# Sorting products and skip connection of a graph network: scaling, attention vectors and bias on other engines

## What is computed

```python
def _L0_gnn_ref(x, edge_index, W_gat, att_src, att_dst, gat_bias, bn_gamma, bn_beta, W_skip, b_skip):
    identity = x @ W_skip + b_skip
    h = (x @ W_gat).reshape(N, H, C)              # N 1250, H 8, C 64
    a_src = jnp.einsum('nhc,hc->nh', h, att_src)
    a_dst = jnp.einsum('nhc,hc->nh', h, att_dst)
    ...                                            # softmax over edges, sum, batch norm, gelu
    return out + identity
x = _layernorm(x + _L0_gnn_ref(x, edge_index, ...), axis=-1)
```

## Time and profile before

| | us |
|---|---|
| median of 3 runs (lowest, highest) | 2041.71 (2039.19, 2046.14) |
| the profiled execution, device time | 2038.94 |
| its span, first to last instruction | 2036.9 |

### The profile page before, as it was taken

The page is one execution under the profiler, slowest core; times in us unless marked ns, Lnnn a source line. Parts: engine busy times, 40 slices in busy tenths (PEclk is TensorE's granted clock), DMA queues, the critical chain, the costliest instruction groups (busy, mean ns, idle before and its releaser), DMA issues.

```text
span 2036.9 us, 21846 instructions
## 1 busy us (share of the span) xinstructions
PE 1693.8 (83%) x5296; PEld 870.4 (43%) x5296; DVE 1607.7 (79%) x3252; ACT 895.4 (44%) x1833; POOL 527.2 (26%) x597
## 2 busy tenths in 40 slices
PE   2668888788387777479999999999598998999997
PEld 1445545533133333444444444457353443444443
DVE  9997899889899999789999999987665754762222
ACT  0112555666355454457777777763204423441100
POOL 4777870044000000045455555520000000002000
PEclk9788999988698899789999999998799999999999
DMA  5101000123210010154545454530010111111000
GB/s 166 10 6 8 6 5 1 36 101 110 103 39 35 32 42 0 56 150 140 151 135 155 133 154 136 153 74 1 25 42 21 62 62 62 58 56 52 0 25 25
DMA packets 66428, 133.78 MB, mean 66 GB/s; under 512 B 19156, under 2 KB 22752, under 8 KB 66385
## 3 DMA queue, kind: packets, MB, share of 16 engines
q1 hardware_dynamic: 40561, 70.33, 11.1%
q0 software_dynamic: 22080, 56.10, 10.3%
q10 hardware_dynamic: 3744, 6.82, 0.9%
HBM read 117.78 MB, written 15.24 MB: 65 GB/s over the span
## 4 chain that ended last, share of the span: by engine, by line
DVE 39%; PE 38%; issue 15%; DMA 4%; DVEq 3%; ACT 2%; SPq 0%; POOL 0%; ACTq 0%; POOLq 0%
PE PS L954 15%; DVE arena L1492 5%; PE PS L922 4%; PE PS L1002 4%; DVE arena L1608 4%; PE PS L738 3%; DVE arena L1488 3%; DVE arena L1353 3%; DVE arena L1604 3%; DVE arena L1611 2%; DVE arena L1614 2%; DVE arena L1352 2%; DVE arena L1383 2%; PE PS L998 2%; PE PS L990 2%
## 5 line engine op out<-in xcount | busy, mean ns | idle before, releaser
L852 PE MATMUL PS<-arena 128*125 128x512 f32 x832 | 397.1, 600 | 20.4 <-ACT arena L1196 20.3
L954 PE MATMUL PS<-arena 128*125 128x512 f32 x720 | 314.5, 600 | 12.2 <-ACT arena L1262 6.6
L1195 ACT ACTIVATE arena<-arena,gslot 128x128 f32<-128x128 f32 x624 | 204.4, 390 | 136.6 <-DVE arena L1608 129.0
L800 PE MATMUL PS<-arena 125*128 125x512 f32 (+1 forms) x480 | 196.3, 552 | 79.0 <-DVE arena L1492 78.9
L597 POOL DMA_INDIRECT arena<-xup,gidx x208 | 218.1, 1048 | 88.4 <-issue 50.0
L561 POOL DMA_INDIRECT recs<-arena x170 | 211.1, 1242 | 62.1 <-issue 47.7
L852 PEld LDWEIGHTS PS<-arena 128*125 128x125 f32 x832 | 152.2, 188 | 157.5 <-issue 101.3
L954 PEld LDWEIGHTS PS<-arena 128*125 128x125 f32 x720 | 136.8, 190 | 189.3 <-issue 189.3
L847 PE MATMUL PS<-w4r,h3r 128*128 128x512 f32 x211 | 168.2, 797 | 10.3 <-DVE h3r L1627 10.3
L800 PEld LDWEIGHTS PS<-arena 125*128 125x128 f32 x480 | 90.3, 199 | 185.1 <-DVE arena L1492 102.4
L1148 ACT ACTIVATE arena<-arena,c 125x1250 f32<-125x1250 f32 x80 | 107.0, 1337 | 137.6 <-DVE arena L1488 137.4
(11 more groups left out here) (235 smaller groups left out, 2905.9 us busy)
## 6 DMA issues: line engine op xcount, KB each, us to landing
arena<-in_spline_wT SPq DMA_DIRECT2D x16, 1024.0 KB, 5.3
arena<-h_rows SPq DMA_DIRECT2D x104, 128.0 KB, 3.4
arena<-uv_rows SPq DMA_DIRECT2D x18, 610.4 KB
h_rows<-arena ACTq DMA_DIRECT2D x26, 256.0 KB, 2.1
arena<-as_rows SPq DMA_DIRECT2D x8, 610.4 KB
arena<-xup,gidx POOLq DMA_INDIRECT x208, 4.2
recs<-arena POOLq DMA_INDIRECT x170, 2.6
x_sb<-in_x SPq DMA_DIRECT2D x1, 2500.0 KB
```

Source lines behind the costliest of these rows:

```text
L800: ins = t.matmul(PS[:, 3 * par + q, 0:n1 - n0], hs[:, sblk, par * C:par * C + 2 * C], wt[:, sblk % WR, n0:n1], start=(sblk == 0), stop=(sb ...
L852: ins = t.matmul(PS[:NP, 2 + 2 * par + q, :], w[:, k, :], prod[:, k, q * 512:(q + 1) * 512], start=(k == 0), stop=(k == GT - 1))
L954: ins = t.matmul(PS[:NP, b, :], basis[:, slot, (k * HB + b) * NP:(k * HB + b + 1) * NP], w_sp[:, slot, k * D:(k + 1) * D], start=(first an ...
L1195: A(pr[:, 4 + m, :], pr[:, 8, :], ACT.Copy, scale=y[:, 1 + m:2 + m])
```

## The change

Five things are changed.

1. Sort rounds: VectorE writes one plain one-hot of the lane per column (`lane_oh`, a new tile), the tile one-hot, and then 6 of the 10 `lane_src` tiles as one-hot times source. ScalarE writes all 10 `lane_dl` tiles and the other 4 `lane_src` tiles (`ACT_SRC = 4`) as a copy with a per-partition scale (`scale_lanes`). `sort_batch` waits for both engines.
2. wa: TensorE transposes W_gat in rounds 4 and 5, ScalarE copies it to `wgT`, and 16 products with 16 columns in round 6 give wa. The attention vectors are loaded into a zeroed block layout `att_d` by 16 DMAs of 64 four-byte pieces.
3. The first layer's blocks run one round later (b = j - 5), and one row part moves behind the rounds.
4. Skip: VectorE adds the identity to W_skip once, in round 10; the bias is a row in a zeroed tile, added by a fifth product with ones; ScalarE copies the sum from PSUM over `x_sb`. Both additions of VectorE go.
5. `cnt_d` is cleared by GpSimd at the start; some semaphores of the loads are joined.

```diff
@@ sync
-            sp.dma_start(att_b[:, 0, :], bass_row(a["L0_gnn_att_src"].rearrange("h c -> (h c)"), 128)).then_inc(s_wg_in, 16)
-            sp.dma_start(att_b[:, 1, :], bass_row(a["L0_gnn_att_dst"].rearrange("h c -> (h c)"), 128)).then_inc(s_wg_in, 16)
+            for q, name in enumerate(("L0_gnn_att_src", "L0_gnn_att_dst")):
+                for h in range(H):
+                    p0 = (h % 2) * C
+                    sp.dma_start(att_d[p0:p0 + C, h // 2, q * H + h:q * H + h + 1], a[name][h:h + 1, :].rearrange("h c -> c h"))\
+                      .then_inc(s_w0_in, 16)
+            sp.dma_start(b_rows[0:1, :], a["L0_gnn_b_skip"].rearrange("(a n) -> a n", a=1)).then_inc(s_w0_in, 16)
@@ gpsimd
+            pool.memset(att_d, 0.0)
+            pool.memset(b_rows, 0.0)
+            pool.memset(cnt_d[:], 0).then_inc(s_const0, 1)
@@ tensor
             def sort_batch(j):
                 pe.wait_ge(s_sort_ok, j + 1)
+                pe.wait_ge(s_lane_cp, j + 1)
+            def w_transposed(c):
+                if c >= 2:
+                    pe.wait_ge(s_wa_cp, c - 1)
+                for k in range(KT):
+                    ins = t.transpose(PS[:, 2 + c % 2, k * 128:(k + 1) * 128], w_gat[:, k, c * 128:(c + 1) * 128], ident[:])
+                ins.then_inc(s_wt_ps, 1)
             for j in range(ROUNDS):
                 sort_batch(j)
-                b = j - 4
+                b = j - 5
+                if j == 4:
+                    pe.wait_ge(s_w0_in, 16 * (3 + 2 * H))
+                    w_transposed(0)
+                    w_transposed(1)
+                if j == 5:
+                    w_transposed(2)
+                    w_transposed(3)
+                if j == 6:
+                    pe.wait_ge(s_wa_cp, KT)
+                    for m in range(KT):
+                        for c in range(KT):
+                            ins = t.matmul(PS[:, 2, m * 2 * H:(m + 1) * 2 * H], wgT[:, c, m * 128:(m + 1) * 128], att_d[:, c, :],
+                                           start=(c == 0), stop=(c == KT - 1))
+                    ins.then_inc(s_wt_ps, 1)
...
-                if j >= ROUNDS - 2:
-                    row_part(j - (ROUNDS - 2))
+                if j == ROUNDS - 1:
+                    row_part(0)
+            row_part(1)
             row_part(2)
+            def skip_block(b):
+                if b >= 2:
+                    pe.wait_ge(s_skip_cp, b - 1)
+                t.matmul(PS[:NP, 6 + b % 2, :], ones[:, 0:NP], b_rows, start=True, stop=False)
+                for k in range(KT):
+                    ins = t.matmul(PS[:NP, 6 + b % 2, :], xT[:, k, b * NP:(b + 1) * NP], w_skip[:, k, :], start=False, stop=(k == KT - 1))
+                ins.then_inc(s_skip_ps, 1)
@@ scalar
+            def scale_lanes(j):
+                act.wait_ge(s_lane_ok, j + 1)
+                if j >= 2:
+                    act.wait_ge(s_order_ps, j)
+                for n in range(SB):
+                    r, c = (j % 2) * SB + n, j * SB + n
+                    ins = A(lane_dl[:, r, :], lane_oh[:, r, :], ACT.Copy, scale=dl1[:, c:c + 1])
+                    if n >= SB - ACT_SRC:
+                        ins = A(lane_src[:, r, :], lane_oh[:, r, :], ACT.Copy, scale=rec[:, c, R_SRCF:R_SRCF + 1])
+                ins.then_inc(s_lane_cp, 1)
-            for b in range(NB + 1):
+            for j in range(ROUNDS):
+                scale_lanes(j)
+                b = j - 5
+                if j in (4, 5):
+                    w_transposed(2 * (j - 4))
+                    w_transposed(2 * (j - 4) + 1)
+                if j == 6:
+                    act.wait_ge(s_wt_ps, KT + 1)
+                    A(wa[:].rearrange("p k n -> p (k n)"), PS[:, 2, 0:KT * 2 * H], ACT.Copy).then_inc(s_wa_cp, 1)
+                if b < 0 or b > NB:
+                    continue
                 if b < NB:
                     act.wait_ge(s_xt_ps, b + 1)
                     A(xT[:, :, b * NP:(b + 1) * NP],
...
+            for b in range(NB):
+                count_groups(4 * b, 2)
+                act.wait_ge(s_skip_ps, b + 1)
+                A(x_sb[:, b, :], PS[:NP, 6 + b % 2, :], ACT.Copy).then_inc(s_skip_cp, 1)
@@ vector
                 for n in range(SB):
-                    v.tensor_scalar(lane_src[:, r, :], iota_src[:NP, 0:128], lane, rec[:, c, R_SRCF:R_SRCF + 1], ALU.is_equal, ALU.mult)
-                    v.tensor_scalar(lane_dl[:, r, :], iota_src[:NP, 0:128], lane, dl1[:, c:c + 1], ALU.is_equal, ALU.mult)
-                    ins = v.tensor_scalar(tile_oh[:, r, :], iota_src[:NP, 0:NT], tile_f[:, c:c + 1], None, ALU.is_equal)
+                    ins = v.tensor_scalar(lane_oh[:, r0 + n, :], iota_src[:NP, 0:128], lane_f[:, c0 + n:c0 + n + 1], None, ALU.is_equal)
+                ins.then_inc(s_lane_ok, 1)
+                for n in range(SB):
+                    v.tensor_scalar(tile_oh[:, r0 + n, :], iota_src[:NP, 0:NT], tile_f[:, c0 + n:c0 + n + 1], None, ALU.is_equal)
+                dve.wait_ge(s_lane_ok, j + 1)
+                for n in range(SB - ACT_SRC):
+                    ins = v.tensor_scalar(lane_src[:, r0 + n, :], lane_oh[:, r0 + n, :], rec[:, c0 + n, R_SRCF:R_SRCF + 1], None, ALU.mult)
                 ins.then_inc(s_sort_ok, 1)
-                if j == 8:
-                    gat_vectors()
+                if j == 10:
+                    dve.wait_ge(s_w0_in, 16 * (3 + 2 * H))
+                    for k in range(KT):
+                        d = w_skip[:, k, k * 128:(k + 1) * 128]
+                        v.tensor_tensor(d, d, ident[:], ALU.add)
-            link(v.memset(cnt_d[:], 0))
-                v.tensor_tensor(x_sb[:, b, :], x_sb[:, b, :], PS[:NP, 6 + b % 2, :], ALU.add).then_inc(s_skip_cp, 1)
-                v.tensor_tensor(x_sb[:, b, :], x_sb[:, b, :], b_skip_b, ALU.add)
```

More of the change, by code:

```diff
@@ L29 @@
 WR = 5
+ACT_SRC = 4
 LEAD = 2
@@ L149, in build @@
         assert o[0] <= 12000
-        b_skip_b = at(12000, [NP, D])
+        b_rows = at(12000, [128, D])
         xT = at(13000, [128, KT, N])
         w_gat, w_skip = at(18000, [128, KT, D]), at(20048, [128, KT, D])
-        att_b = at(22096, [128, 2, D])
+        att_d = at(22096, [128, KT, 2 * H])
+        wgT = at(26000, [128, KT, D])
         h_sb = at(23120, [NP, NB, D])
@@ L172, in build @@
         dl1 = at(5800, [NP, EC])
+        lane_oh = at(10620, [NP, 2 * SB, 128], f16)
         lane_src = at(1020, [NP, 2 * SB, 128], f16)
@@ L256, in build @@
         s_basis_ok = sem("s_basis_ok")
-        s_bn_in = sem("s_bn_in")
         s_bn_ok = sem("s_bn_ok")
@@ L342, in build @@
         s_sort_ok = sem("s_sort_ok")
+        s_lane_ok = sem("s_lane_ok")
+        s_lane_cp = sem("s_lane_cp")
+        s_wt_ps = sem("s_wt_ps")
         s_sp_free = sem("s_sp_free")
@@ L365, in build @@
         s_w4_ok = sem("s_w4_ok")
-        s_wa_ok = sem("s_wa_ok")
+        s_wa_cp = sem("s_wa_cp")
         s_wdiag_zero = sem("s_wdiag_zero")
-        s_wg_in = sem("s_wg_in")
-        s_wk_in = sem("s_wk_in")
+        s_w0_in = sem("s_w0_in")
         s_wl2_in = sem("s_wl2_in")
         s_wl3_in = sem("s_wl3_in")
-        s_wm_in = sem("s_wm_in")
+        s_small_in = sem("s_small_in")
         s_wrep_ok = sem("s_wrep_ok")
@@ L421, in _ @@
             sp.dma_start(x_sb[:], a["x"].rearrange("(b p) n -> p b n", p=NP)).then_inc(s_x_in, 16)
[L422 to L428 removed]
+            sp.dma_start(w_gat, kview(a["L0_gnn_W_gat"])).then_inc(s_w0_in, 16)
+            sp.dma_start(w_skip, kview(a["L0_gnn_W_skip"])).then_inc(s_w0_in, 16)
+            sp.wait_ge(s_wdiag_zero, 1)
+            for q, name in enumerate(("L0_gnn_att_src", "L0_gnn_att_dst")):
[4 more added lines that the diff above has]
+            sp.dma_start(b_rows[0:1, :], a["L0_gnn_b_skip"].rearrange("(a n) -> a n", a=1)).then_inc(s_w0_in, 16)
             for q in range(2):
[L430 to L432 removed]
+                sp.dma_start(w_m1[q * 8:q * 8 + 8, q * HID:(q + 1) * HID], a["L1_gnn_W_mlp1"]).then_inc(s_small_in, 16)
+                sp.dma_start(w_m2[q * HID:(q + 1) * HID, q * HID:(q + 1) * HID], a["L1_gnn_W_mlp2"]).then_inc(s_small_in, 16)
+                sp.dma_start(w_m3[q * HID:(q + 1) * HID, q * HID:(q + 1) * HID], a["L1_gnn_W_mlp3"]).then_inc(s_small_in, 16)
             for q, name in enumerate(("L0_gnn_gat_bias", "L0_gnn_bn_gamma", "L0_gnn_bn_beta")):
[L434 removed]
+                sp.dma_start(bnp[:, q, :], a[name]).then_inc(s_small_in, 16)
             sp.wait_ge(s_rows_cp, 3)
@@ L700, in row_part @@
                 if q == 0:
-                    pe.wait_ge(s_wa_ok, 1)
+                    pe.wait_ge(s_wa_cp, KT + 1)
                 if q == 2:
@@ L740, in count_groups @@
                         ins.then_inc(s_cnt_ps, 1)
+            def skip_block(b):
[5 more added lines that the diff above has]
+                ins.then_inc(s_skip_ps, 1)
             for b in range(NB):
                 count_groups(4 * b, 2)
-                node_block(b, w_skip, s_skip_ps, s_skip_cp)
+                skip_block(b)
```

(33 more changed lines are left out.)

6 lines of the change are left out of this document (1 added, 5 removed).

## The result

The changed kernel takes 2102.6 us in the median (2100.4 to 2105.3, 4 runs) against 2042.5 us for the kernel before on the same chip (4 runs, one more than in the table above): a ratio of 1.029, 95% interval 1.027 to 1.032, 60 us slower. 2088 us was forecast, with a range of 2062 to 2108. The profiled execution has a span of 2098.7 us, 61.8 us more than before.

The account below looks back on a forecast made before the run. VectorE was taken to bound the sort rounds, a loop through three engines the counting. 45.5 us for a later counting start plus 3 in counting gave +48.5 on 2038.9; with 2.8 for the median, 2088 us, range 2062 to 2108.

Parts of the forecast that it names:

- the favoured case: Sort rounds: TensorE and ScalarE alternate with a falling clock; 2088 us, own range 2078 to 2098, chance 0.67.
- Where it stands: Sort rounds from round 6: ScalarE's products queue behind its copy of h, so TensorE and ScalarE alternate; 10.6 us against 7.3.
- ScalarE's share: Sort rounds: ScalarE's 14 products by a per-partition column take 0.29 us each, 4.1 us a round, 4.2 with the tail.
- The clock: Sort rounds: TensorE's 4.8 us gap lets its clock fall, 2.45 us charged to 8 of 10 rounds; 12.6 us a round.
- Rival 1: Sort rounds: the clock stays up through the 4.8 us gaps, nine rounds of 10.6 us; 2069 us, chance 0.13.
- The way to round 7: Sort start through round 6: TensorE's first batch starts at 52.3 us, round 7's products are done at 90.9; weights cost nothing.
- rival 2: Round 4: the attention pieces land late and TensorE stands 17 us; 2105 us, chance 0.10.
- End of the sort: Round 16 begins at 204 us, counting 25.5 us after it at 229.5, 45.5 us later; cnt_d clearing costs 0 to 2.
- Counting: Counting blocks: bias product adds 0.86 us each, VectorE's additions lie inside its wait, scatter relief -4.3; +3 us in all.
- Rival 4: Counting blocks follow TensorE's own work, 12.9 us; 28 us less than forecast, 2060 us, chance 0.04.
- Rival 3: Sort rounds: ScalarE's products run beside TensorE's round, whose length is the longest of 5.3, 5.2 and 5.8 us; 2031, chance 0.06.
- Everything after is the same work, moved: Stages after counting: the same work only starts later, with no further cost.

Follow-up runs that it names:

- Experiment 1: Changed kernel with ScalarE's products of round j+1 ahead of the copies of x and h of round j: 2025.5 us, ratio 0.991 to the kernel before.
- experiment 3: Changed kernel with ACT_SRC = 0, so VectorE makes all 10 source tiles and ScalarE 10 products a round: 2088.4 us, ratio 1.022 to the kernel before.
- experiment 5: Changed kernel with five unread f32 products on TensorE after the f32 products of rounds 6 to 15: 2084.8 us, ratio 1.021 to the kernel before.
- experiment 2: Changed kernel with cnt_d cleared by VectorE after the sort rounds, not by GpSimd at the start: 2096.1 us, ratio 1.025 to the kernel before.
- experiment 4: Changed kernel with four skip products again and the bias added by VectorE after ScalarE's copy: 2095.3 us, ratio 1.0248 to the kernel before.
- experiment 7: Kernel before the change without VectorE's 20 skip additions, skip products still made: 2038.2 us, ratio 0.9987 to the kernel before.

## Why the prediction was right, and by how much it was short

*The number.* 2102.6 us lies in the range of 2062 to 2108, but 4.6 us above the 2078 to 2098 that the favoured case had for itself; the mechanism held and its price was too low. The sum has a slip as well: 2038.9 + 48.5 + 2.8 is 2090, not 2088. The times given for the rivals are 2 to 3 us too low in the same way; nothing hangs on it.

*Where it stands.* Right, and the heart of the matter. The gap came out at 4.86 us where the sum had 4.8. Experiment 1 shows the order to be the cause, experiment 3 gives the dose.

*ScalarE's share.* Right: 0.29 us from start to start for f16 tiles too (the last seven of a round start between 36.56 and 38.31 us). The Trainium skill, ScalarE: Activation LUTs, section "What ACT_TABLE_LOAD costs", gives 186 ns + 0.833 ns an element, 93 more for a per-partition operand and an overlap of 93; for 128 columns that is an estimate of 0.29 us, and the trace agrees.

*The clock.* The mechanism was right, the size too small. I charged 2.45 us to 8 rounds of 10, 12.6 us a round; 13.0 was measured; the batches of rounds 7 to 15 all took 3.2 to 3.6 us, where one at 2.4 GHz takes 1.95. That is 3.3 us in nine rounds. The rule that I weighed against the rows, of the Trainium skill, TensorE: Matmul & The Clock Gate, section "HAM oscillation — how this bites in real kernels", that a wait between bursts lets the clock fall each time, gave 13.1 and was the better number; the trace agrees, with all ten batches from round 7 on slow. Rival 1 is out: the clock did not stay up through the gaps, and experiment 5 shows that it does once they are filled.

*The way to round 7.* Here a term was mis-sized. I set the clearing on GpSimd at 0 to 2 us; it cost 7.7 us at the first sort instruction, and 6.5 between the medians of experiment 2 and the changed kernel. I looked at where GpSimd's own program had room and not at what its clearing does to VectorE beside it, though the stretching of VectorE by the scatters (1.14) stood in its first paragraph. Round 7 began at 95.0 and not 90.9, so 3.6 us were won back on the way. The first four rounds gave 0.7 of them, round 4 gave 2.3, since its batch and transposes ran at 2.4 GHz (1.94 and 1.04 us) where the sum had 1.2 GHz, and round 5 gave 0.8. In round 6 the narrow products took 3.9 us, not 5.0, but the f32 products after them lost as much to the clock. That was in part luck: in experiment 5's trace the same program took 7 us longer to the same place. The weights were there in time: the first transpose follows its batch at once (61.10 us), so rival 2 is out, though the 17 small transfers took 1.15 us each to issue (30.51 to 50.07 us), not the 0.6 of the sum; they began 7 us earlier than it assumed.

*End of the sort.* 25.5 us were expected from round 16 to counting; the first group came 27.8 after it against 22.5 before: 5.3 us more, where the sum had 5.6 (3.5 and 2.1). The third row part cost 3.4 us and the batch at the low clock 1.3.

*Counting.* Right for the block: 0.86 us more (14.87 to 15.73) and nothing for VectorE's additions (experiments 4 and 7). In all it is +4.2 us where the sum had +3, because the relief from the scatters was put too high: the four blocks that now stand beside them are 6.4 us longer together than four others, and before eight were 9.6 us longer, so 3.2 us are saved and not 4.3. Rival 4, blocks of TensorE's own 12.9 us, is out: the waits of 1.78 and 0.68 us stayed. Rival 3, the two engines side by side, isn't how the changed kernel runs, but it is how experiment 1 does, and there a round is 5.65 us where the rival had 5.8.

*Everything after is the same work, moved.* This step was 4.8 us short (57.1 at the last counting group, 61.8 at the end). Part is seen: a stretch of 45.34 us of TensorE's products behind 1508 us was 43.95 before, with a mean clock of 0.93 in place of 0.96. What moved the clock there I have not tried, and one execution on each side can't tell it from chance; 15 executions of the kernel before on one chip lie between 2038.5 and 2045.2 us.

The misses, 4.1 us on the way to round 7, 3.3 of the clock, 1.2 in counting and 4.8 behind it, are 13.4 us, and 48.5 + 13.4 is the 61.8 of the trace within rounding.

## What to carry to other kernels

An engine's program is a queue: before you hand an engine a job that another waits for each round, look at what stands ahead of it. If that is a wait for the same engine's end of round, the two alternate, and moving the job one wait forward was worth 77 us here, more than everything the change moved. Work taken from an engine that already waits in each block bought next to nothing (13.7 us of additions: 2.4), while one product of 0.86 us added on the loop cost its full length in each block.

## What the runs showed of the hardware

A clearing on GpSimd stopped VectorE's f32 comparisons until it ended: ten comparisons took 1.67 us alone, 3.92 beside a clearing of 5.30 us and 9.49 beside one of 10.50. It was the first of the ten that stood, with 2.50 and 8.08 us; the other nine followed at their usual pace. The nine instructions with two tensor inputs just before them (`scalar_tensor_tensor`, 125 x 170 f32) were not held: they took 3.35 us, 3.30 in the kernel before, although the clearing ran beside the last 2.5 us of them. The clearing goes by elements: 12500 two-byte ones took 10.50 us, the same bytes as 6250 words 5.30.

The Trainium skill, GPSIMD Engine Reference, section "8. Key points", says that the two engines share their SBUF interfaces and contend when VectorE runs in a two-port mode or has two inputs in SBUF. The trace agrees that they contend, doesn't show in which mode the comparisons ran, and differs on the two inputs, which cost nothing beside this clearing.

A gap of 4.86 us on TensorE let the clock fall: the granted clock of the batch behind it was 0.50 (107.28 to 110.70 us). Gaps of 3.69 us in experiment 3 did so too, and the batches behind them in rounds 7 to 16 took 3.1 to 3.6 us, not 1.95; but one batch there, in round 6, took 1.94 us behind a gap of 3.78. Through the gaps of 0.57 us of experiment 5 the clock stayed at 1.00.
